# Local attention of a two-layer transformer block: the order of work in the steps that fill the pipeline

## The reference, cut to what matters

```python
h = shift_token(x)                     # the second half of each row is taken from the row above
q, k, v = split(h @ wqkv, 3)           # 3 x 512 columns
q = l2norm(q) * qs ; k = l2norm(k) * ksc
q, k = rotary_xpos(q, k)               # q*cos*scale + rotate_half(q)*sin*scale ; k with 1/scale
sim = einsum('bhwid,bhwjd->bhwij', q_window * 8, own and previous window of k)
sim = where(i < j or i > j + 128 or j == -1, -big, sim)
out = softmax(sim) @ v ; x = x + out @ wo
```

## Time and profile before

| | us |
|---|---|
| median of 3 runs | 4440.74 (4437.42 to 4447.78) |
| profiled execution | 4442.02 |
| its span, first to last instruction | 4440.4 |
| busy in it: PE, DVE, ACT, POOL | 3952.2, 3372.9, 2531.6, 1223.5 |
| local attention of the first layer, in the trace | 854 to 1316 |
| local attention of the second layer | 1534 to 1996 |

### The profile page before, as it was taken

The page is one execution under the profiler, slowest core; times in us unless marked ns, Lnnn a source line. Parts: engine busy times, 40 slices in busy tenths (PEclk is TensorE's granted clock), DMA queues, the critical chain, the costliest instruction groups (busy, mean ns, idle before and its releaser), DMA issues. The chain is left out here.

```text
span 4440.4 us, 97994 instructions
## 1 busy us (share of the span) xinstructions
PE 3952.2 (89%) x39572; PEld 2282.1 (51%) x39572; DVE 3372.9 (76%) x5488; ACT 2531.6 (57%) x3400; POOL 1223.5 (28%) x967
## 2 busy tenths in 40 slices
PE   7999999589989879999976999999999999857995
PEld 4888888356655546665543322332333333444763
DVE  5688888678875478875597899999998987465454
ACT  3566666455544245544323667787888888415562
POOL 1123231367751167751141000000000000123554
PEclk9999999799999989999987899999999999857997
DMA  1011010133320033320054000000000000114444
GB/s 61 12 32 40 29 37 11 32 70 63 61 51 11 6 70 63 59 43 27 15 126 72 14 11 4 11 3 4 10 4 11 4 11 7 46 40 132 88 105 96
DMA packets 311476, 176.70 MB, mean 40 GB/s; under 512 B 221892, under 2 KB 302488, under 8 KB 310424
## 3 DMA queue, kind: packets, MB, share of 16 engines
q1 hardware_dynamic: 278680, 124.51, 13.1%
q0 software_dynamic: 13440, 21.24, 2.7%
q10 hardware_dynamic: 18944, 25.17, 1.7%
HBM read 83.64 MB, written 42.25 MB: 28 GB/s over the span
## 5 line engine op out<-in xcount | busy, mean ns | idle before, releaser
L2187 DVE TENSOR_REDUCE s_tops<-ps 128x2 f32<-128x1024 f32 (+3 forms) x1152 | 1251.1, 1131 | 143.8 <-PE ps L2073 103.1
L2156 ACT ACTIVATE s_weights<-ps 128x1024 f32<-128x1024 f32 (+3 forms) x1152 | 1093.8, 953 | 343.6 <-PE ps L2086 192.2
L2108 PE MATMUL ps<-s_weights,v_flat 128*32 128x256 f32 (+1 forms) x8704 | 692.5, 390 | 7.3 <-ACT s_o_t L2162 5.9
L2067 PE MATMUL ps<-keys,s_q 48*128 48x512 f16 (+3 forms) x2304 | 435.9, 376 | 46.1 <-DVE s_tops L2187 24.5
L2086 PE MATMUL ps<-s_q,keys 50*128 50x512 f16 (+3 forms) x2304 | 434.2, 374 | 47.5 <-DVE s_tops L2187 33.3
L2223 POOL CAST s_shift<-s_minus_top 128x16 f16<-128x16 f32 x32 | 6.3, 196 | 1429.8 <-DVE s_minus_top L2194 1429.8
L582 PE MATMUL ps<-a_qt,a_kt 128*128 128x256 f16 x3072 | 375.4, 273 | 3.8 <-POOL s_ones L537 3.8
L2086 PEld LDWEIGHTS ps<-s_q,keys 50*128 50x128 f16 x2304 | 112.4, 93 | 512.0 <-issue 254.0
L1208 PE MATMUL ps<-attention_w,la_yt 128*128 128x512 f16 x1152 | 289.7, 399 | 57.0 <-DMA la_yt<-la_y_parts 49.5
L1283 ACT ACTIVATE la_weights<-ps 128x1024 f32<-128x1024 f32 x124 | 126.9, 1023 | 349.7 <-PE ps L1198 349.7
L582 PEld LDWEIGHTS ps<-a_qt,a_kt 128*128 128x128 f16 x3072 | 301.0, 98 | 40.2 <-POOL s_ones L537 4.2
(11 more groups left out here) (357 smaller groups left out, 7388.4 us busy)
## 6 DMA issues: line engine op xcount, KB each, us to landing
ex_w_whole<-in_L_ffn_w_dram ACTq DMA_DIRECT2D x16, 1024.0 KB, 7.2
qk_parts<-a_parts SPq DMA_DIRECT2D x64, 128.0 KB, 3.1
attention_w<-attention_split SPq DMA_DIRECT2D x3, 2048.0 KB, 7.3
keys<-qk_parts SPq DMA_DIRECT2D x48, 128.0 KB, 5.4
s_q<-qk_parts SPq DMA_DIRECT2D x48, 128.0 KB, 4.5
x<-in_x_dram SPq DMA_DIRECT2D x8, 512.0 KB, 9.0
la_table<-in_rotary_dram SPq DMA_DIRECT2D x64, 64.0 KB, 2.1
a_table<-in_rope_dram POOLq DMA_DIRECT2D x8, 512.0 KB, 5.4
```

The source lines that it names most:

```text
L2067: mm = pe.matmul(m.ps[:, bank, 0:width], b.q[rows(half, KEY_PARTS * L1_DH), place % 2, pair, t * P:(t + 1) * P], m.keys[rows(half, KEY_PAR ...
L2108: mm = pe.matmul(m.ps[h * QUAD:(h + 1) * QUAD, OUT, begin:end], m.v_flat[:, first:first + QUAD], weights[:, a % 2, h, begin:end], start=(k ...
L2156: act.activation(weights[:, a % 2, 2 * pair:2 * pair + 2, skip:CHUNK], m.ps[:, bank:end + 1, skip:CHUNK], ACT.Exp).then_inc(s["exp"], 1)
L2187: dve.tensor_reduce(tops[:, u % 2, :, i % 2, t, c], m.ps[:, bank:end + 1, 0:width], AX.X, ALU.max).then_inc(s["max"], 1)
```

## The change: what it does

A helper `filling(step)` is true for steps below 0. In those steps four engines take another order; in all steps from 0 on the order is as before.

```diff
+        def filling(step):
+            return step < 0
@@ POOL
                 def norms(w):
                     pool.wait_ge(s["ss"], w + 1)
+                    after(pool, s["qk"], w)
                     pool.tensor_tensor(rnorm[:, :], ss[:, :], ..., ALU.pow)
                 def step(i):
+                    if exists(i + 4) and filling(i):
+                        tables(i + 4)
                     if exists(i + 3):
                         normalise(i + 3)
-                    if exists(i + 4):
+                    if exists(i + 4) and not filling(i):
                         tables(i + 4)
@@ PE
                 def step(i):
+                    if exists(i + 4) and filling(i):
+                        project_q(i + 4)
+                        project_k(i + 4)
                     if exists(i + 2):
                         find(i + 2, 0)
-                    if exists(i + 4):
+                    if exists(i + 4) and not filling(i):
                         project_q(i + 4)
...
-                    if exists(i + 4):
+                    if exists(i + 4) and not filling(i):
                         project_k(i + 4)
@@ ACT
-                    if exists(i + 3):
+                    if exists(i + 3) and not filling(i):
                         high(i + 3)
                     if exists(i + 4):
                         square(i + 4)
+                    if exists(i + 3) and filling(i):
+                        high(i + 3)
@@ DVE
                 def step(i):
+                    if filling(i):
+                        if exists(i + 4):
+                            rotate(i + 4)
+                        if exists(i + 3):
+                            low(i + 3)
+                        if exists(i + 4):
+                            sums(i + 4)
                     if exists(i + 2):
                         find(i + 2, 0)
...
                     if exists(i + 2):
                         find(i + 2, 1)
                         take_shift(i + 2)
-                    if exists(i + 3):
+                    if exists(i + 3) and not filling(i):
                         low(i + 3)
-                    if exists(i + 4):
+                    if exists(i + 4) and not filling(i):
                         rotate(i + 4)
...
-                    if exists(i + 4):
+                    if exists(i + 4) and not filling(i):
                         sums(i + 4)
```

## The result

| | before | after |
|---|---|---|
| median of 11 runs each, same chip (lowest to highest), us | 4439.06 (4432.26 to 4447.78) | 4455.85 (4448.93 to 4462.34) |
| ratio, 95% interval | | 1.0039 (1.0030 to 1.0048) |
| profiled execution, us | 4442.02 | 4458.89 |
| its span | 4440.4 | 4457.2 |
| busy PE, DVE, ACT, POOL | 3952.2, 3372.9, 2531.6, 1223.5 | 3960.6, 3375.0, 2530.1, 1220.4 |

The change made the kernel slower by 17.3 us (4439.06 times 0.0039; 13.3 to 21.3); the two medians are 16.8 apart. The forecast was 4457, by +16.4. PE is busy 8.4 us more, but 8.2 of them lie behind the second local attention, in instructions that the change doesn't touch (2155.65 us from 2009.40 to the end, for 2147.50 from 1996.00 before). What the change does shows in waits, in the filling steps of each layer.

A forecast was written before the change was run, and what follows sets the result against it. PE bounds the full steps, so only the start of step 0, find(2, 0), counts. Two layers by 8.2 us give +16.4 on 4442.0, 4458.4, or 4457 us against the median; own range 4453 to 4463, with rivals 4446 to 4465.

The forecast's parts named there:

- low held by the add: Filling steps: DVE's low stands still while POOL adds, lasting about 3 us; low(0) ends at 879.72, norms(1) at 881.13.
- rival B: DVE and POOL don't hold each other in the new place; find(2) 4.4 us late per layer, +8.8, 4450; chance 0.16.
- The searches behind sums(2), and the finds of tile 0 in series: Tile 0's searches wait on DVE for sums(2), 892.24; find(0, 1) waits for them until 893.2, take_shift(0) at 895.0.
- turn_k(1) behind turn_shift(0) on SP: SP's list: turn_k(1), data ready at 890.99, waits until 896.55; find(1, 0) at 901.15, 7.15 us late.
- find(2, 0) at 915.35: Start of step 0 on PE, first layer: 8.2 us later than 907.15, bounds 6.9 and 9.9; second layer the same.
- rival E: POOL's add(3), second to low(2), is held 1.1 us, and the clock stays at 1.2 GHz: 9.9 us per layer, 4461; chance 0.10.
- The wait before find(2, 0): Sign in the changed profile: a DMA wait of some 8 us on PE before find(2, 0).
- Nothing gives it back: Steps from step 0 on are PE's, so the late start passes to the end: two layers by 8.2 us, +16.4.
- Rival D: Step 0 starts late but later steps take it up; within 4 us of now, 4443; chance 0.10.
- Rival C: The searches don't decide, so find(2) follows its own shorter chain: 2 to 11 us less, 4433; chance 0.08.
- The added wait: POOL's norms(w) waits for normalise(w-1): priced at nothing, bounds 0 and 0.1 us per filling tile, at most 0.6.

The follow-up runs named there:

- Experiment 3: The changed kernel with POOL's add of tiles 1 to 3 cut to 64 of 1024 columns; +9.3 us against the kernel before.
- experiment 1: The changed kernel with DVE's list alone back in its old order; +5.3 us against the kernel before.
- experiment 9: The kernel before with ten unread reductions on DVE in step -1 ahead of the search of find(1, 0); +14.2 us against the kernel before.
- experiment 2: The changed kernel with SP issuing turn_k and turn_q of tile i+3 before turn_shift of tile i+2 in filling steps; +8.4 us against the kernel before.
- experiment 6: The kernel before with only POOL's new order (tables first, added wait) and ACT's (square first); +2.2 us against the kernel before.
- experiment 10: The kernel before with, in filling steps, DVE's sums before rotate and POOL's norms before add, plus the added wait; -4.0 us against the kernel before.
- experiment 7: The kernel before with only the added wait in norms, in all tiles; +0.9 us, ratio 1.0002.
- experiment 8: The changed kernel with sums before low on DVE in filling steps; +10.7 us against the kernel before.

## Why the prediction was right, step by step

Times are given with the 0.56 us added, next to the forecast.

- **low held by the add.** `low(0)` ends at 879.63 (879.72 forecast), norms(1) at 881.04 (881.13), norms(2) at 892.22 (892.40). Experiment 3 takes the hold away: `low` is 1.23, and lateness falls by 6.4 us over two layers, where the distance between forecast and rival B was 7.6.
- **The searches behind sums(2), and the finds of tile 0 in series.** `find(0, 1)` at 893.03 (893.2), `turn_shift(0)` at 895.06 (895.4). Experiments 1 and 9 show it from both sides: without the late searches most of the loss goes, and with a late search alone it comes.
- **turn_k(1) behind turn_shift(0) on SP.** 896.24 (896.55), and `find(1, 0)` at 900.87 (901.15). Right as an account of this schedule, incomplete as a cause: experiment 2 shows that with SP's order mended the same searches hold step 0 by PE's and ACT's lists.
- **find(2, 0) at 915.35.** It came at 915.52, 8.37 late (8.2 forecast), and 8.62 in the second layer. Two terms on the way were off and cancelled. `project(3)` was taken at 4.7 us, between its bounds of 4.10 and 5.28; it took 4.03, so that `rotate(3)` began at 898.91 instead of 899.8. And `add(3)` was held by `low(2)` for 0.9 us, 3.25 for 2.35: rival E's event, for which the forecast had nothing. The clamp that waits for it ended at 904.69, forecast 904.7. That these two cancel to a few hundredths is luck; each is worth 0.9 us. E's whole sum needed a project of 5.28 us as well, and didn't get it.
- **The wait before find(2, 0)** is 5.31 us, not some 8: a projection of 2.70 us at 906.95 lies in the gap. That had no part in the sum.
- **Nothing gives it back.** +17.3 us for 17.0 of lateness in the timed runs, with an interval of 13.3 to 21.3. That the two agree so closely is in part luck: in the profiled pair the span is 16.8 longer, but that is 17.0 of lateness, less 2.3 in the steps of the two layers, less 1.3 ahead of the first and between the two, plus 3.4 behind the second, in instructions that nobody changed. Over the eleven kernels of the table a line through zero has a slope of 0.92 (the sum of the products over the sum of the squares of the lateness). That most of the lateness reaches the end is shown; that all of it does is not. Rival D, within 4 us of now, is out for the change. Experiment 2 lies under that line with an interval that still reaches it (12.9); experiment 6 doesn't reach it (6.2, where the line has 8.8), and why stays open.
- **Rival C**, the searches don't decide, is out by experiments 1 and 9. (Its "2 to 11 us less" has one layer's 1.9 us as its lower end; over two layers that is 3.8.) Its counterpart is true, though: with searches left alone the shorter chain is worth 3.6 us of earliness (experiment 10).
- **The added wait** at nothing: experiment 7 agrees (-3.1 to 4.9 us).
- **Two readings of the trace fall short, and neither changed the sum.** The prediction has no row of a POOL operation held as the second. The trace before holds one, in the last steps of each layer: `low` starts first, and POOL's multiply, 1.16 us in the earlier trace rows, lasts 1.67. Rival E's event could have been priced from it.

```profile
1279.83 1.23 DVE L1368 TENSOR_TENSOR la_parts<-la_straight,la_parts 128x1024 f16<-128x1024 f32 x1 [0.47 <-ACT la_parts L1308]
```

```profile
1280.39 1.67 POOL L1113 TENSOR_TENSOR la_ot<-la_o,la_ot 128x512 f16<-128x512 f32 x1 [1.68 <-ACT la_ot L1302]
```

And the reduction at 867.14 and the rotation of the earlier trace rows start before POOL's operation, so that their normal durations say nothing of being held; a first one never is. That POOL's second operation isn't held there either, 2.34 and 1.16 us, is what speaks for it. In the change both start second: the reduction of tile 3 at 901.82 under the add of 900.85 to 904.10, in 1.21 us, and the rotation of tile 2 at 884.32 under a multiply of 884.19 to 886.09, in 1.23.

Not tried: PE's order put back alone. By reading the lists, the kernel would never end: `find(0, 1)` would wait for a search that stands on DVE behind the rotation of tile 2, whose projection would stand behind that find on PE.

## What to carry to other kernels

In a hand-written pipeline, look not at what a moved step gains but at what now stands behind it on each in-order list, and follow that until it reaches the row where the full steps begin. A later start of the full steps costs nearly its whole length once for each fill (a slope of 0.92 here), however full the engines are afterwards. When two chains meet at one issue, shortening one pays only down to the other: here 4.5 us on the norms of tile 1 bought 1.5 to 2.1 at `find(2, 0)`.

## What the runs showed of the hardware

The hold between DVE and POOL follows one rule in each pair below, in both directions: the second operation ends as if it had begun about 0.15 us before the first one ended.

| second | first | alone | ends after the first | difference |
|---|---|---|---|---|
| low, 128x1024 (after) | add | 1.22 | 1.08 | 0.14 |
| clamp, 128x16 (experiment 8) | add | 0.17 | 0.03 | 0.14 |
| add, 128x1024 (after) | low | 2.35 | 2.21 | 0.14 |
| add, 128x64 (experiment 3) | low | 0.32 | 0.17 | 0.15 |
| power, 128x16 (experiment 8) | low | 2.93 | 2.77 | 0.16 |

That is a lock, not a slowing down: how long the second waits doesn't depend on its own size, and a clamp of 16 columns waits for an add of 1024. Not every DVE operation is held: in the change the sums of tile 3 started under an add and took their 1.21 us, and the rotation of tile 2, one of whose inputs is in PSUM, started under a multiply and took 1.23. The Trainium skill, page SBUF — State Buffer, section "Who interferes with whom", has the second in issue order fully blocked, whichever engine it is; the table agrees, but for the 0.15 us. The prediction had weighed this rule by one row (1.42 for 1.22) and called the hold less than whole; by five pairs it is whole, and the 0.15 us looks like a part of an operation that runs ahead of the lock. That last is my reading of the times; no run here tests it.
